# Layer 1's sums in tiles of their own, its rows loaded a block ahead, and routing steps laid between bn_stats

## The reference

```python
x = x + _L0_gnn_ref(_ln(x), adj, ...)      # scores, mask, softmax over 64 nodes, weighted sum
x = x + _L0_ffn_ref(_ln(x), ...)           # router over 8 experts, top 2, own layer norm, gelu, hidden 512
x = x + _L1_gnn_ref(_ln(x), adj, ...)      # the same with a relu behind the sum
x = x + _L1_ffn_ref(_ln(x), ...)           # router on _ln(x), top 2, gelu, hidden 256
```

## Time and profile before

| | us |
|---|---|
| median of three runs | 943.96 |
| the three runs | 937.42, 943.96, 946.27 |
| the profiled execution, device time | 937.9 |
| its span in the trace | 936.0 |
| busy in the span: PE, DVE, POOL, ACT | 711.8, 723.5, 546.9, 491.9 |
| granted TensorE clock, mean share of full speed | 0.876 |

### The profile page before, as it was taken

One profiled execution on the slowest core, in us unless ns is written; L12 is line 12 of the kernel. 1 busy time (PEld: TensorE's weight loads), 2 busy tenths in 40 slices (PEclk: granted clock), 3 DMA queues, 4 the chain that ended last, 5 costly groups with the idle time before them and its releaser, 6 DMA issues.

```text
span 936.0 us, 24539 instructions
## 1 busy us (share of the span) xinstructions
PE 711.8 (76%) x6599; PEld 563.6 (60%) x6600; DVE 723.5 (77%) x2663; ACT 491.9 (53%) x1113; POOL 546.9 (58%) x544
## 2 busy tenths in 40 slices
PE   3888877567999999999988887886277877777500
PEld 2666555363899999999556765765236765555400
DVE  6788889762799999999388899997517777787538
ACT  2455665410677777777136566565306655555234
POOL 0037777776277667767400567777764777777720
PEclk9977978857999999999999699798589999999855
DMA  8394333331233323324534454332333333333757
GB/s 228 94 189 116 106 99 95 96 106 61 70 91 87 87 81 85 87 81 136 165 112 125 137 145 150 91 91 74 99 92 100 100 105 99 96 102 99 240 226 321
DMA packets 129399, 111.47 MB, mean 119 GB/s; under 512 B 30306, under 2 KB 112681, under 8 KB 129352
## 3 DMA queue, kind: packets, MB, share of 16 engines
q1 hardware_dynamic: 112072, 77.04, 29.9%
q0 software_dynamic: 17280, 33.87, 11.0%
HBM read 60.32 MB, written 52.36 MB: 120 GB/s over the span
## 4 chain that ended last, share of the span: by engine, by line
PE 35%; DVE 25%; issue 19%; POOL 12%; DMA 5%; ACT 2%; SPq 1%; POOLq 1%; DVEq 0%; ACTq 0%
PE bank L631 10%; PE bank L645 10%; POOL row_buf L457 6%; POOL y_buf L465 6%; PE bank L520 3%; DVE xin L973 3%; DVE stat L912 3%; PE bank L569 2%; PE bank L617 2%; PE bank L517 2%; PE bank L501 2%; DVE x1w L1009 2%; DVE x1w L1013 2%; PE bank L687 1%; DMA xin<-x_buf 1%
## 5 line engine op out<-in xcount | busy, mean ns | idle before, releaser
L457 POOL DMA_INDIRECT row_buf<-pay,slot x256 | 253.4, 990 | 217.8 <-DVE slot L1079 139.7
L465 POOL DMA_INDIRECT y_buf<-g_y,g_dst x284 | 293.3, 1033 | 132.1 <-issue 87.1
L806 ACT ACTIVATE g_xT<-bank 128x512 f16<-128x512 f16 x142 | 84.7, 597 | 171.9 <-PE bank L617 169.0
L631 PE MATMUL bank<-g_xT,w 128*128 128x256 f16 x1278 | 165.8, 276 | 1.5 <-ACT g_xT L806 1.4
L569 PE MATMUL bank<-cst,tri 128*128 128x512 bf16 x518 | 120.2, 388 | 24.9 <-DVE w L1189 14.0
L631 PEld LDWEIGHTS bank<-g_xT,w 128*128 x1278 | 117.6, 99 | 18.6 <-issue 2.1
L569 PEld LDWEIGHTS bank<-cst,tri 128*128 128x128 bf16 x518 | 51.4, 100 | 83.9 <-issue 29.3
L645 PE MATMUL bank<-w,g_h 128*128 x1260 | 84.4, 219 | 17.7 <-DVE g_y L1234 17.7
L813 ACT ACTIVATE xn<-bank,b_cols 128x256 f32<-128x256 f32 x216 | 86.7, 474 | 20.2 <-PE bank L631 11.9
L813 ACT ACTIVATE xt<-bank,b_cols 128x256 f32<-128x256 f32 x210 | 84.4, 475 | 14.0 <-PE bank L631 10.7
L645 PEld LDWEIGHTS bank<-w,g_h 128*128 128x128 f16 x1260 | 76.1, 98 | 25.6 <-issue 23.1
(11 more groups left out here) (191 smaller groups left out, 1312.9 us busy)
## 6 DMA issues: line engine op xcount, KB each, us to landing
g_in<-row_buf SPq DMA_DIRECT2D x142, 130.0 KB, 2.2
yin<-y_buf SPq DMA_DIRECT2D x20, 512.0 KB, 5.7
x_buf<-x1w SPq DMA_DIRECT2D x16, 520.0 KB, 5.4
xin<-x_buf SPq DMA_DIRECT2D x10, 520.0 KB, 5.3
y_buf<-g_y,g_dst POOLq DMA_INDIRECT x284
xin<-in_x_dram SPq DMA_DIRECT2D x8, 512.0 KB, 5.2
adj_in<-in_adj_dram SPq DMA_DIRECT2D x16, 256.0 KB, 3.4
row_buf<-pay,slot POOLq DMA_INDIRECT x256, 2.3
```

What stands on the lines that cost most here:

```text
L457: pool.indirect_dma_start(row_buf[L][:, :], bass.IndirectOffsetOnAxis(ap=slot[q][:, k, t:t + 1], axis=0), pay[q][:, t, :], None).then_inc( ...
L465: pool.indirect_dma_start(y_buf[L][:, :], bass.IndirectOffsetOnAxis(ap=g_dst[k][:, t:t + 1], axis=0), g_y[k][:, t, :], None, bounds_check= ...
L631: last = nc.tensor.matmul(dst, w[:, bass.ds(e * (2 * HID[L]) + (wp * HID[L] + c * P), P)], g_xT[q][:, xp, :], start=(m == 0), stop=(m == 2))
L806: nc.scalar.activation(g_xT[q][:, :, :], x_ps[q], ACT.Copy).then_inc(s.gT_sb, 1)
```

## The change

Three things.

- In layer 1 the sums x + results go to tiles of their own, `x_sum = [h_new, fin_e]`, and what read them in `xin` reads them there: the statistics, ACT's xn, the second add and x1w. (Both tiles were used before only at the very end of the kernel.)
- With `xin[q]` free once the second result is added, layer 1's x rows of block n + 3 are loaded together with its adjacency and results, behind `taken`; the load behind `x_done` is left to layer 0.
- The first `statistics` of a step (`braid=True`) has a pause behind each of its first seven bn_stats, in both layers; the second one is as before. In layer 1 `route` lets one pause pass before it waits for the logits, where it let three pass.

```diff
+WAIT_LOGITS = 1
...
+        x_sum = [h_new, fin_e]
...
                         sp.wait_ge(s.taken, n + 2)
+                        if L == 1:
+                            load_x(L, n + 3, (q + 1) % 2)
                         load_early(L, n + 3, (q + 1) % 2)
-                    if not isinstance(n, int) or 0 <= n < NBLK - 2:
+                    if L == 0 and (not isinstance(n, int) or 0 <= n < NBLK - 2):
                         sp.wait_ge(s.x_done, n + 1)
                         load_x(L, n + 2, q)
...
-                normalise(xn, xin[q][:, :, X_AT:X_END], rstd1, nmr1, SL[L].xn_ready)
+                normalise(xn, xin[q][:, :, X_AT:X_END] if L == 0 else x_sum[q][:, :, :], rstd1, nmr1, SL[L].xn_ready)
...
-            def statistics(src, rstd, nmr, beside, std=None, both=None):
+            def statistics(src, rstd, nmr, beside, std=None, both=None, braid=False):
...
                 for t in range(TILES):
                     last = V.bn_stats(stat[:, t, :], src[:, t, :])
+                    if braid and t < TILES - 1:
+                        pause()
                 ch.did(last)
                 pause()
...
-                    last = V.scalar_tensor_tensor(xin[q][:, t, X_AT:X_END], yin[q][:, k, t, :], xin[q][:, t, k:k + 1],
-                                                  xin[q][:, t, X_AT:X_END], ALU.mult, ALU.add)
+                    so_far = xin[q][:, t, X_AT:X_END] if k == 0 else x_sum[q][:, t, :]
+                    last = V.scalar_tensor_tensor(x_sum[q][:, t, :], yin[q][:, k, t, :], xin[q][:, t, k:k + 1],
+                                                  so_far, ALU.mult, ALU.add)
...
-                                                      xin[q][:, t, X_AT:X_END], ALU.mult, ALU.add)
+                                                      x_sum[q][:, t, :], ALU.mult, ALU.add)
...
-                    for _ in range(3):
+                    for _ in range(WAIT_LOGITS):
                         yield
                     dve.wait_ge(s.lg_copied, n + 1)
```

More of the change, by code:

```diff
@@ L1086, in statistics_of @@
                     if has_input:
-                        statistics(xin[q][:, :, X_AT:X_END], rstd1, nmr1, beside, std=std1[q] if L == 0 else None).then_inc(s.st1, 1)
+                        statistics(xin[q][:, :, X_AT:X_END] if L == 0 else x_sum[q][:, :, :], rstd1, nmr1, beside, std=std1[q] if L == 0 else None, braid=True).then_inc(s.st1, 1)
                     finish_steps(beside)
```

## The result

| | before | changed |
|---|---|---|
| median, us | 940.43 | 947.43 |
| lowest and highest | 936.84, 946.27 | 941.78, 959.75 |
| profiled execution, device time | 937.9 | 948.43 |
| its span | 936.0 | 946.5 |
| busy PE, DVE, POOL, ACT | 711.8, 723.5, 546.9, 491.9 | 714.7, 726.2, 550.9, 492.6 |

A forecast was written before the change was run, and what follows sets the result against it. Bound: a chain through DVE and PE in both layers' block stretches, with POOL's stores beside it. Terms 1.85 + 0.36 + 3.1 − 0.79 = +4.5 us gave 942.4 (profiled) or 948.5 (median); 946 was taken, range 938 to 955.

The forecast's parts named there:

- Braid, layer 0: Term: DVE's chain from first bn_stats to L1057 in layer 0 grows 0.37 us a block, +1.85 over five blocks.
- A wait costs nothing: Rival, chance 0.15: in both layers each op takes the same however followed; +2.3 us left, 940 to 946.
- Slots(4): Block 4's slots in layer 0, with which the end of POOL's stores was said to move: +1.85 us.
- Braid, layer 1: Term: the same DVE chain in layer 1 grows 0.06 us a block, +0.36 over six blocks.
- Late logits: Term: layer 1's earlier logits' wait stalls DVE in two blocks behind long half-clock spells, +3.1 us together.
- x rows: Term: early x loads remove DVE's three waits at layer 1's adds, 1.1 us, of which −0.79 counts.
- The end moves with slots(5): Step: layer 1's end shifts with block 5's slots, as POOL waits for slots up to block 5.
- POOL as the bound from block 6: Step: in layer 1 POOL's indirect stores, not their slots, set the pace from block 6; 0.30 us behind the store before.
- Logits late in nearly every block: Rival, chance 0.15: stalls shift layer 1's blocks against clock spells; four to six late blocks, +8 to +12 us, 947 to 957.
- The clock holds: Rival, chance 0.12: PE's shorter rest before x_done prevents long half-clock spells in layer 1; no late logits, −1.2 us, 937 to 943.
- ScalarE was no bound: Step: ScalarE's xn, though starting later behind nmr, is done before PE needs it after x_done: no cost.

The follow-up runs named there:

- e4: Changed kernel with only layer 0 braided, each route-step wait behind the next bn_stats, and three pauses before the logits' wait: 937.22 us, 0.9969 of before.
- e2: Changed kernel with the braid in layer 0 alone and three pauses before the logits' wait: 939.96 us, 0.9996 of before.
- e5: The changed kernel run again, nothing edited, on a second chip: 947.66 us, 1.0096 of before.
- e7: Kernel before plus both braids and the early logits' wait, without the new buffers and early x rows: 948.57 us, 1.0099 of before.
- e6: Changed kernel, both braids kept, with the logits' wait moved behind all eight bn_stats and the first stage after them: 940.51 us, 1.0021 of before.
- e1: Changed kernel with only the buffers and early x rows, no braid, three pauses before the logits' wait: 941.66 us, 0.9998 of before.
- e9: Changed kernel with five more filler matmuls a block (13 for 8) behind layer 1's attention: 940.32 us, 1.0002 of before.
- e10: Changed kernel with four pauses instead of one before the logits' wait, so behind the fifth bn_stats: 939.50 us, 0.9981 of before.
- e11: e8 with five more filler matmuls a block (13 for 8) behind layer 1's attention: 937.51 us, 0.9964 of before.
- e3: Changed kernel with the braid in layer 1 alone, early logits' wait kept: 942.70 us, 1.0025 of before.
- e12: The edit of e3 run once more, on a third chip: 942.57 us, 1.0021 of before.
- e8: e4 with one pause instead of three before layer 1's logits' wait, still behind all eight bn_stats: 935.88 us, 0.9965 of before.

## Why the prediction was right, and where it was not

**Sum and range.** +4.5 was forecast, +5.9 was measured. From the time of the profiled execution the forecast gave 942.4, from the median of three 948.5; 946 was taken between, and 947.4 came. The median of 22 runs of before is 940.4, so the base under the 946 was about 1 us too high and the change 1.4 (by the medians 2.5) too low: that the two times are so close is in part luck. The parts hold less well than the sum.

**Braid, layer 0 (+0.37 a block).** Measured +0.37 to +0.55 (6.77 to 6.95 against 6.40; the mean of six blocks is 6.88, and 6.44 before), and single bn_stats 0.45 apart, where 0.44 was worked out. The price of a wait, 0.25 behind a 64 wide step, was right. *A wait costs nothing* fell, and with it the reading of the Trainium skill's "VectorE: DVE Perf Modes", "The DRAIN you can't avoid", by which a semaphore costs nothing extra (measured there on a row of eight copies); for the small operations of this kernel it doesn't hold. e4 shows how much of the price can be covered: a route step whose wait stands behind the next bn_stats adds 0.13, and one whose wait stands ahead of it 0.26 (0.32 and 0.45 against 0.19). Slots(4) end 1.6 later, with +1.85 expected, and the stores end 3.4 later, with some 2 expected; in e2, where layer 0's braid is alone, they end 2.1 later, but its time of 0.9996 shows no cost. So the term is seen in the trace and not in the time of that kernel, whose interval just takes it in. In e2's profile DVE waits 6.0 us for PE's scores in layer 0, in those of before and of the change 12.0 and 12.1.

**Braid, layer 1 (+0.06 a block).** +0.07 to +0.09 (6.44 and 6.46). That is against the 6.37 of the earlier trace rows; two of the six blocks of before take 6.50 and 6.55. Right, and too small to matter.

**Late logits (+3.1).** Two late blocks were forecast at 1.74 and 1.67, both behind long spells at half clock. Two came, of 1.85 and 1.47, behind such spells, but in other blocks: the spells had moved, from 517 and 589 to 546 and 618. e5 has two, e7 three. That a block behind such a spell is late by 1.5 to 1.8 was right; that there would be two was read from one trace, and met by luck as much as by reason. This was the best step, and e6 shows that it carries the largest part of the loss.

**x rows (−0.79).** The waits are gone (527.81 begins behind 527.69, with no idle time):

```profile
527.81 2.19 DVE L981 SCALAR_TENSOR_TENSOR fin_e<-yin,xin 128x128 f32<-128x128 f32 x8
```

e1 measures 0.9998, which neither shows nor excludes −0.8. The loads behind `taken` did no harm.

**"The end moves with slots(5)".** This step failed in the profiled execution. Slots(5) are 3.6 us late, of which two stalls and six braids make 1.85 + 1.47 + 0.5 = 3.8. But the end is 7.1 late, because slots(6) came so late that POOL waited 2.80 for them. POOL as the bound from block 6 was read from one trace, and held only as long as the chain kept its old distance from it. A stall isn't needed for that: in e2 and e6, which have none, POOL waits 2.88 and 2.68 there.

**What was missing.** The forecast added stalls as though each cost its own length, and left the clock as it was. Against that stand e9 (a full stall is still there, the loss is not) and e10 (stalls a third shorter, the whole loss gone), with the limits said there. Theory F, that a stall costs more than its length where it brings the next spell closer, would fit e9, but as it was put on record it missed e10 (1.009 expected) and was not borne out by e11. The rival *Logits late in nearly every block* had the mechanism, stalls that shift blocks against spells, but at four to six stalls; two or three came. That three of seven stalls were followed by an early spell is seen; that the stall causes it is not shown.

**The clock holds.** This rival said that the shorter rest ahead of `x_done` would end the spells. The rest did get shorter, to 1.72 us where the earlier trace rows had 3.22, and the spells stayed. But a rest that the rival hadn't counted opened in its place, ahead of the fillers that wait for `st1`: 2.12 and 2.08 in two of the six blocks, where it was at most 0.58. So the change doesn't test what the rival said of PE's rests as a whole; e9, which fills that rest, comes nearer to it.

```profile
593.47 0.20 PE L551 MATMUL bank<-hot_any,tri 128*128 128x64 bf16 x1 [1.72 <-DVE x1w L1021]
...
612.26 1.90 PE L574 MATMUL bank<-cst,tri 128*128 128x512 bf16 x8 [2.08 <-DVE nmr L956]
```

ScalarE was no bound either, as said: its xn, behind nmr, ends at 522.58, before DVE's x1w (522.98).

```profile
519.39 3.19 ACT L714 ACTIVATE xn<-h_new,nmr,rstd 128x128 f32<-128x128 f32 x8 [0.50 <-DVE nmr L956]
```

**What stays open.** Layer 0's braid alone costs nothing that could be measured (e2), layer 1's alone 0.21 to 0.25%, both together 0.63 to 0.99%. The table has, for each kernel, the ratio, the stalls of over 1 us and the sum of the six blocks' times from the first bn_stats to the low parts in layer 1's profile, and the mean granted clock of its runs (share of full speed) with that of the kernel before on the same chip.

| | ratio | stalls | six blocks, us | clock (before) |
|---|---|---|---|---|
| before | 1 | 0 | 38.5 | |
| change | 1.0063 | 2 | 42.3 | 0.871 |
| e5, the change again | 1.0096 | 2 | 42.3 | 0.869 (0.875) |
| e7, no buffers | 1.0099 | 3 | 44.1 | 0.868 (0.875) |
| e3, braid in layer 1 | 1.0025 | 1 | 40.9 | 0.870 (0.872) |
| e12, e3 again | 1.0021 | 1 | 41.0 | 0.874 (0.873) |
| e9, change and fillers | 1.0002 | 1 | 40.6 | 0.883 (0.873) |
| e10, wait 4 | 0.9981 | 2 | 39.1 | 0.878 (0.873) |
| e6, wait 8 | 1.0021 | 0 | 37.5 | 0.876 (0.875) |
| e2, braid in layer 0 | 0.9996 | 0 | 38.6 | 0.880 (0.872) |

Within the runs of the kernel before, 0.01 of clock goes with 3.1 to 3.7 us on each of the three chips. By that the clock would hide 2 to 3 us in e2, give back 3 to 4 in e9 and 2 in e10, and add 2 to 3 in e5 and e7. That is an estimate from runs that merely vary together; it would bring the parts nearer to their sum. Why the clock differs from kernel to kernel isn't shown. The start of layer 1 may be the link from layer 0: with the braid of layer 0 and its wait ahead of bn_stats, layer 1's first add starts at 467.4 to 471.7 (seven profiles, mean 469.7), with no braid there at 466.0 to 467.9 (four, mean 467.2), and with e4's braid at 467.4 to 469.2. No run moved that start by itself, and the change was not run beside e9 and e10, so neither was tried.

## What to carry to other kernels

Price an interleaving by its waits: a step laid between two independent operations cost 0.13 us here with its wait behind the second one and 0.26 with it ahead, where it cost 0.25 alone; only the first gains anything. A wait for another engine goes as late in the queue as its consumer allows, above all when fill work that would cover it is queued behind it; the slack of the arrival in a single trace, 0.7 us here, says little if that engine's clock changes. If a change creates stalls, their cost may differ from their sum: compare the clock of all runs and not only the one profile, and run the edits beside the change on the same chip.

## What the runs showed of the hardware

- Eight bn_stats of 128 elements run 0.19 us apart. With a 64 wide step between them they are 0.32 apart if the wait stands behind the next bn_stats, and 0.45 if it stands ahead. The instructions are the same; only the place of the wait differs. Of the 0.26 that such a step adds, one independent operation covers half.
- The time of a kernel may depend on work of PE that computes nothing: 1.0063 for the change and 1.0002 with five more filler matmuls a block (e9, on another chip); between e8 and e11, which have no stalls, the same matmuls made no difference that shows (0.9965 and 0.9964).
- The mean granted clock of a kernel's runs differs between kernels that compute the same: 0.868 (e7) to 0.883 (e9), with 0.872 to 0.875 before.
- In layer 1, spells of some 10 us at half clock begin 44 us or more apart where DVE doesn't stall (the last one left out), and 24 us apart behind three of twelve stalls of over 1 us. In layer 0 of e4 they come 21 us apart without any stall. In the ten microseconds ahead of the spell at 618 of the change, PE's longest rest is 2.08 us.
